# Folding a layer norm into the matrix product behind it: relu output transposed, row statistics added as a product of six rows

## The reference

```python
h = jax.nn.relu(hypergraph_conv(x, adj, W1, b1))   # [512, 512] per graph
h = layer_norm(h, gamma, beta)                     # the inner norm, called Z in the kernel
y = hypergraph_conv(h, adj, W2, b2)                # starts with xw = h @ W2^T, W2^T is [512, 256]
return y + x
```

## Time and profile before

| | us |
|---|---|
| median of 3 runs (range) | 1648.58 (1648.41 to 1649.86) |
| the profiled execution: its own time | 1649.85 |
| the profiled execution: span of the trace | 1648.0 |
| PE busy | 1486.1 (90%) |
| DVE busy | 1146.0 (70%) |
| ACT busy | 908.8 (55%) |
| POOL busy | 284.7 (17%) |
| one turn of the loop | 96.10 |

### The profile page before, as it was taken

How to read it: one execution, slowest core, us unless ns; L and a number is a source line. 1 busy time by engine, 2 the same in 40 slices (tenths; PEclk the granted TensorE clock), 3 DMA queues, 4 the chain that set the end, 5 groups by cost and what they waited for, 6 DMA issues and landing times.

```text
span 1648.0 us, 26778 instructions
## 1 busy us (share of the span) xinstructions
PE 1486.1 (90%) x9850; PEld 1085.8 (66%) x9850; DVE 1146.0 (70%) x2522; ACT 908.8 (55%) x1517; POOL 284.7 (17%) x348
## 2 busy tenths in 40 slices
PE   5688888899899999999999999999999999998986
PEld 4676666667666676766667676666767666676633
DVE  6564766758678686777868677786867778676663
ACT  3424555365565546556554655656465565646564
POOL 3111020202112030210303021030302103120001
PEclk9788999999999999999999999999999999999998
DMA  7010111112120211212021121202112121110021
GB/s 222 1 58 13 52 39 58 39 39 84 58 78 16 74 59 45 76 57 76 15 75 56 45 76 57 76 15 73 58 45 76 57 76 38 45 64 26 1 64 52
DMA packets 58550, 92.17 MB, mean 56 GB/s; under 512 B 4288, under 2 KB 23296, under 8 KB 58496
## 3 DMA queue, kind: packets, MB, share of 16 engines
q1 hardware_dynamic: 58496, 91.44, 17.1%
HBM read 83.04 MB, written 8.39 MB: 55 GB/s over the span
## 4 chain that ended last, share of the span: by engine, by line
PE 55%; issue 20%; DVE 16%; ACT 6%; POOL 2%; DMA 1%; SPq 0%; DVEq 0%; ACTq 0%; POOLq 0%
PE ring_f L1299 33%; PE ring_b L1299 9%; PE ring_b L1569 6%; PE pv_acc L1585 3%; DVE att L1133 3%; DVE bns L928 3%; PE ring_f L1468 2%; POOL rstd L489 2%; DVE rows L1030 2%; ACT hf L568 1%; DVE uz L952 1%; ACT rows L606 1%; DVE m L957 1%; DVE xc_s L952 1%; PE ring_f L1435 1%
## 5 line engine op out<-in xcount | busy, mean ns | idle before, releaser
L1133 DVE TENSOR_TENSOR att<-ring_b,at 128x1024 f32<-128x1024 f32 x256 | 307.2, 1219 | 77.1 <-PE ring_b L1569 69.7
L710 ACT ACTIVATE att<-att 128x1024 f32<-128x1024 f32 x256 | 265.1, 1054 | 136.2 <-DVE att L1133 135.2
L489 POOL TENSOR_TENSOR rstd<-var,mhalf 128x4 f32<-128x4 f32 x80 | 81.3, 1017 | 769.6 <-DVE var L943 769.6
L1299 PE MATMUL ring_f<-w,uz 128*128 128x256 f32 (+1 forms) x896 | 188.9, 333 | 2.3 <-DVE uz L952 1.7
L1299 PE MATMUL ring_f<-m,tr_h 128*128 128x256 f32 x1024 | 190.4, 287 | 0.0
L1299 PEld LDWEIGHTS ring_f<-m,tr_h 128*128 128x128 f32 x1024 | 158.9, 191 | 32.8 <-issue 32.1
L1299 PEld LDWEIGHTS ring_f<-w,uz 128*128 128x128 f32 x896 | 152.0, 192 | 29.8 <-DVE uz L952 12.2
L1585 PE MATMUL pv_acc<-att,xp_n 128*32 128x512 f32 x1024 | 138.5, 617 | 33.9 <-ACT att L710 26.8
L1569 PE MATMUL ring_b<-xc_t,xp_t 32*128 32x512 f32 x1024 | 147.6, 646 | 20.9 <-DVE att L1133 11.7
L1299 PE MATMUL ring_f<-m,inc_n 128*128 128x256 f32 x1024 | 132.2, 288 | 17.8 <-POOL m L493 16.3
L1299 PEld LDWEIGHTS ring_f<-m,inc_n 128*128 128x128 f32 x1024 | 127.0, 195 | 30.6 <-issue 18.7
(11 more groups left out here) (161 smaller groups left out, 2767.8 us busy)
## 6 DMA issues: line engine op xcount, KB each, us to landing
at<-in_adjT SPq DMA_DIRECT2D x32, 1024.0 KB, 5.6
rows<-in_adjT SPq DMA_DIRECT2D x16, 1024.0 KB, 5.5
adj_n<-in_adj SPq DMA_DIRECT2D x16, 1024.0 KB, 5.5
x_in<-in_x SPq DMA_DIRECT2D x16, 512.0 KB, 3.8
out_x<-h SPq DMA_DIRECT2D x16, 512.0 KB, 6.6
wrow<-in_adj SPq DMA_DIRECT2D x16, 256.0 KB, 6.0
att<-in_Wk SPq DMA_DIRECT2D x3, 256.0 KB, 4.2
att<-in_W1T SPq DMA_DIRECT2D x1, 512.0 KB, 9.2
```

The lines of the kernel that those rows point to most:

```text
L489: pool.tensor_tensor(rstd[k][:], var[k][:], mhalf[:], ALU.pow).then_inc(rstd_made[k].sem, 1)
L710: act.activation(v, v, ACT.Tanh).then_inc(tanh_made.sem, 1)
L1133: dve.tensor_tensor(att[:, u % 2, 2 * half:2 * half + 2], ring_b[half][:], at[:, u % NT].unsqueeze(1).broadcast_to([P, 2, N]), ALU.mult).t ...
L1299: ins = pe.matmul(dst, lhsT, rhs, start=(first and n == 0), stop=(last and n == len(pairs) - 1), skip_group_check=True)
```

## The change

The inner norm is no longer applied before the transposes. With r = relu output, mean m and rstd s of a row, z @ W + beta @ W2 = s * (r @ W - m * (gamma @ W2) + (1/s) * (beta @ W2)), where W is W2 with gamma in it. So:

- `f_z` and, for this norm, `offset` are gone; `f_zT` transposes the relu output and waits for `relu_made`.
- A DVE step `f_stat` makes from `sums`, `var` and `rstd` six columns for each node, high and low parts of -m and of 1/s = var*rstd. A PE step `f_stat` transposes them (four transposes of 128x6 into a PSUM bank), ACT `f_stat` copies 6x512 to `stat_t`. In `xw` the product `stat_t` (6 rows) with `rowz` (6 rows: gamma @ W2 and beta @ W2, high and low) takes the place of `sel` with `rowb`, at the head of the last part (k = 3) and not of the first.
- The eviction of xw multiplies by s: ACT and DVE now handle each tile of 128x256 by itself (`scaled`, `scaled_low` with `rstd[Z]` for the factor), as they do for `m` and `m2`.
- The bank table gets an entry v for the new tile (bank 1, between w and n).
- The setup makes `rowz` instead of the first `rowb`, and `set_up_w2` of ACT stands in `f_zT`.
- The lists of all five engines are written anew. In the loop, the units of attention lie one later against the `f` steps; some lists begin a turn at another place.

```diff
-        BANKS = (0, 2, 1, 0, 2, 1, 0, 2, 1, 0, 2, 1, 0, 2, 1, 0, 2, ...)
+        BANKS = (0, 2, 1, 0, 2, 1, 0, 2, 1, 0, 2, 1, 0, 2, 1, 1, 0, 2, ...)
 # ACT
-            def f_z(g, i):
-                if i == 0 and not seen(g, 1):
-                    set_up_w2()
-                normed(g, rows, rows, Z, i, ACT.Identity)
+            def f_stat(g):
+                act.wait_ge(stat_full.sem, stat_full.after(g, 1))
+                if seen(g, 1):
+                    act.wait_ge(xw_full.sem, xw_full.after(g, 2, ago=1))
+                copy(stat_t[0:6], bank_of(ST, 0)[0:6], stat_copied)
-                copy(m1[:, 0, 2 * k:2 * k + 2].rearrange("p t d -> p (t d)"), bank_of(XW, k)[:], xw_hi)
+                scaled(k, bank_of(XW, k), rstd[Z], lambda t: m1[:, 0, t], xw_hi)
 # DVE
+            def f_stat(g):
+                cols = stat[:].rearrange("p t (a k) -> p a t k", a=2)
+                dve.wait_ge(rstd_made[Z].sem, rstd_made[Z].after(g, 1))
+                if seen(g, 1):
+                    dve.wait_ge(stat_full.sem, stat_full.after(g, 1, ago=1))
+                c_stat.begin()
+                dve.tensor_scalar(pair[:, 0], sums[Z][:, :, 0], -0.5, None, ALU.mult)
+                c_stat.link(dve.tensor_tensor(pair[:, 1], var[Z][:], rstd[Z][:], ALU.mult))
+                here(c_stat, g)
+                dve.tensor_copy(cols[:, :, :, 0], pair[:])
+                c_stat.link(dve.tensor_copy(cols[:, :, :, 1], pair[:]))
+                here(c_stat, g)
+                dve.tensor_tensor(cols[:, :, :, 2], pair[:], cols[:, :, :, 0].bitcast(F32), ALU.subtract)\
+                   .then_inc(stat_made.sem, 1)
+                c_stat.end()
-                low(v[:, 1], bank_of(XW, k)[:], v[:, 0], xw_lo)
+                scaled_low(k, bank_of(XW, k), rstd[Z], lambda t: m1[:, 1, t], lambda t: m1[:, 0, t], xw_lo)
 # PE
-                        pe.wait_ge(h_made[Z].sem, h_made[Z].after(g, i + 1))
+                        pe.wait_ge(relu_made.sem, relu_made.after(g, i + 1))
-                    pairs = [(sel[:], rowb[:, 0])] if ks[0] == 0 else []
+                    pairs = [(stat_t[0:6, i * P:(i + 1) * P], rowz[0:6])] if ks[-1] == HT_ - 1 else []
+            def f_stat(g):
+                pe.wait_ge(stat_made.sem, stat_made.after(g, 1))
+                ps = bank(g, ST, 0)
+                for i in range(NT):
+                    ins = pe.transpose(ps[0:6, i * P:(i + 1) * P], stat[:, i].bitcast(F32), ident[:])
+                ins.then_inc(stat_full.sem, 1)
+                    pe.wait_ge(stat_copied.sem, stat_copied.after(g, 1))
 # PE, list of the loop, from the first convolution to the transposes behind y
-                    (2, k_attend, 3), (2, k_scores, 5), (0, f_conv1, 0), (0, f_conv1, 1), (0, f_conv1, 2),
-                    (0, f_conv1, 3), (2, k_attend, 4), (2, k_scores, 6), (2, k_attend, 5), (2, k_scores, 7),
-                    (0, f_zT, 0), (0, f_zT, 1), (1, k_hT), (0, f_zT, 2), (0, f_zT, 3), (0, f_xw, 0), (0, f_xw, 1),
-                    (0, f_xw, 2), (0, f_xw, 3), (2, k_attend, 6), (0, f_m2, 0), (0, f_m2, 1), (2, k_outT, 0),
-                    (2, k_attend, 7), (0, f_y, 0), (2, k_outT, 1), (0, f_y, 1), (1, k_xp, 0), (1, k_xp, 1),
-                    (1, k_xn, 0), (1, k_xc, 0), (0, f_hT, 0), (0, f_hT, 1), (1, k_xc, 1), (1, k_xn, 1), (0, f_sj),
+                    (2, k_attend, 2), (2, k_scores, 4), (0, f_conv1, 0), (0, f_conv1, 1), (0, f_conv1, 2),
+                    (0, f_conv1, 3), (2, k_attend, 3), (2, k_scores, 5), (0, f_zT, 0), (0, f_zT, 1), (0, f_zT, 2),
+                    (2, k_attend, 4), (2, k_scores, 6), (0, f_zT, 3), (0, f_xw, 0), (2, k_attend, 5), (0, f_xw, 1),
+                    (0, f_stat), (2, k_scores, 7), (0, f_xw, 2), (0, f_xw, 3), (2, k_attend, 6), (1, k_hT),
+                    (0, f_m2, 0), (0, f_m2, 1), (2, k_outT, 0), (2, k_attend, 7), (0, f_y, 0), (2, k_outT, 1),
+                    (0, f_y, 1), (1, k_xp, 0), (1, k_xp, 1), (1, k_xc, 0), (1, k_xc, 1), (1, k_xn, 0),
+                    (1, k_xn, 1), (0, f_hT, 0), (0, f_hT, 1), (0, f_sj), (0, f_q, 0), (0, f_q, 1), (2, k_ax, 0, 0),
 # DVE, list of the loop, the same stretch (graph g stands here as 1, because the turn now begins inside it)
+                    (0, bn, 0, 0), (1, f_conv1, 2), (1, bn, 1, 0), (1, f_conv1, 3), (1, bn, 1, 1), (1, bn, 1, 2),
+                    (3, k_unit, 5, 0), (3, k_unit, 5, 1), (1, f_zT, 0), (1, f_zT, 1), (1, bn, 1, 3),
+                    (1, variance, 1), (1, f_zT, 2), (3, k_unit, 6, 0), (3, k_unit, 6, 1), (1, f_zT, 3),
+                    (1, f_stat), (3, k_unit, 7, 0), (3, k_unit, 7, 1), (1, f_xw, 0), (1, f_xw, 1), (1, f_m2, 0),
 # SP, list of the loop
-                    (0, next_x), (2, next_at), (0, next_wrow), (4, store), (2, next_at2), (0, next_adj),
-                    (0, next_adjt),
+                    (0, next_x), (0, next_wrow), (4, store), (2, next_at), (3, next_at2), (0, next_adjt),
+                    (0, next_adj),
```

More of the change, by code:

```diff
@@ L538, in _ @@
+                (-1, k_y, 3),
             )
@@ new lines, in _ @@
+                (0, k_unit, 4, 0), (0, k_unit, 4, 1), (2, bn, 1, 3), (2, variance, 1), (0, k_unit, 5, 0),
+                (0, k_unit, 5, 1), (2, f_zT, 0), (2, f_zT, 1), (0, k_unit, 6, 0), (0, k_unit, 6, 1),
+                (0, k_unit, 7, 0), (0, k_unit, 7, 1), (2, f_stat), (2, f_zT, 2), (2, f_zT, 3), (2, f_xw, 0),
+                (2, f_xw, 1), (0, k_outT, 0), (0, k_outT, 1), (0, bn, 4, 0), (0, bn, 4, 1), (0, bn, 4, 2),
+                (2, f_m2, 0), (2, f_m2, 1), (0, bn, 4, 3), (0, variance, 4), (1, k_hT), (0, offset, 4),
@@ L1642, in turn @@
+                    (2, k_out, 1), (0, f_tt, 0), (0, f_tt, 1), (0, f_tt, 2), (1, k_scores, 0), (0, f_tt, 3),
+                    (0, f_r1), (0, f_r, 0), (1, k_scores, 1), (0, f_r, 1), (1, k_attend, 0), (0, f_x1),
+                    (1, k_scores, 2), (0, f_x2, 0), (0, f_x2, 1),
                 ))
@@ new lines, in _ @@
+                (2, f_xw, 0), (0, k_attend, 7), (2, f_stat), (2, f_xw, 1), (2, f_xw, 2), (2, f_xw, 3),
+                (0, k_outT, 0), (0, k_outT, 1), (2, f_m2, 0), (2, f_m2, 1), (1, k_hT), (2, f_y, 0), (2, f_y, 1),
+                (1, k_xp, 0), (1, k_xp, 1), (1, k_xn, 0), (1, k_xc, 0), (1, k_xn, 1), (1, k_xc, 1), (2, f_hT, 0),
+                (2, f_hT, 1), (2, f_q, 0), (2, f_q, 1), (2, f_sj), (2, f_q, 2), (2, f_q, 3), (0, k_ax, 0, 0),
+                (0, k_ax, 0, 1), (0, k_ax, 1, 0), (0, k_ax, 1, 1), (0, k_out, 0), (0, k_out, 1), (2, f_tt, 0),
@@ new lines, in _ @@
+                (1, k_scores, 5), (3, f_zT, 3), (3, f_xw, 0), (3, f_xw, 1), (1, k_attend, 4), (1, k_scores, 6),
+                (1, k_attend, 5), (3, f_stat), (1, k_scores, 7), (3, f_xw, 2), (3, f_xw, 3), (3, f_m2, 0),
+                (3, f_m2, 1), (3, f_y, 0), (3, f_y, 1), (2, k_hT), (1, k_attend, 6), (1, k_attend, 7),
+                (1, k_outT, 0), (1, k_outT, 1), (2, k_xp, 0), (2, k_xp, 1), (3, f_hT, 0), (3, f_hT, 1),
+                (2, k_xc, 0), (2, k_xc, 1), (3, f_sj), (3, f_q, 0), (3, f_q, 1), (2, k_xn, 0), (3, f_q, 2),
@@ new lines, in _ @@
+                (-1, f_xw, 0), (-1, f_xw, 1), (-1, f_stat), (-3, k_scores, 7), (-1, f_xw, 2), (-1, f_xw, 3),
+                (-3, k_attend, 6), (-2, k_hT), (-1, f_m2, 0), (-1, f_m2, 1), (-3, k_attend, 7), (-3, k_outT, 0),
+                (-3, k_outT, 1), (-1, f_y, 0), (-1, f_y, 1), (-2, k_xp, 0), (-2, k_xp, 1), (-2, k_xn, 0),
+                (-2, k_xc, 0), (-2, k_xc, 1), (-1, f_hT, 0), (-1, f_hT, 1), (-2, k_xn, 1), (-1, f_q, 0),
+                (-1, f_q, 1), (-1, f_sj), (-1, f_q, 2), (-1, f_q, 3), (-3, k_ax, 0, 0), (-3, k_ax, 0, 1),
@@ L1716, in _ @@
+                (-1, k_scores, 5), (-2, k_out, 1), (-1, k_attend, 4), (-1, k_scores, 6), (-1, k_attend, 5),
+                (-1, k_scores, 7), (-1, k_attend, 6), (-1, k_attend, 7), (-1, k_outT, 0), (-1, k_outT, 1),
+                (-1, k_ax, 0, 0), (-1, k_ax, 0, 1), (-1, k_ax, 1, 0), (-1, k_ax, 1, 1), (-1, k_out, 0),
+                (-1, k_out, 1),
             )
```

656 lines of the change are left out of this document (319 added, 337 removed).

## The result

The changed kernel takes 1614.07 us (median, 1613.27 to 1615.91), the kernel before beside it on the same chip 1649.22: a ratio of 0.9786 with a 95% interval of 0.9774 to 0.9798, 35 us or 2.1% less. The forecast was 1626, its range 1606 to 1652. So the direction and the range held, and the gain is 1.55 times the forecast one: 35 us for 22.6.

What follows compares the result with a forecast made beforehand. PE's own work was taken as the bound, 90.84 of a 96.10 us turn. Ten turns at -1.4 (-14), graphs 2, 3, 4 and 15 (-5.6), graph 0 (-2.0) and graph 1 (-1) gave -22.6, so 1626 us, range 1606 to 1652.

Steps and rivals of the forecast that it cites:

- the waits around z: PE's loop waits of 0.71 for the `pv_acc` copy, 1.53 for a tanh and 0.21 for z; -2.45 us a turn.
- `xp_t`: PE's wait for `xp_t` in the loop, claimed to go because xc follows `xp 1`; -0.78 us a turn.
- The waits that the prediction adds up to 4.98: PE's loop waits: three around z, one for `xp_t`, two at transposes behind y, one for ax's low part; 4.98 us.
- The wait at the statistics step: PE waiting for `stat_made` at the new transposes, between 0 and 0.8 us a turn; 0.4 taken.
- The walk: Convolution to `f_stat` in the new order: PE 11.4 us, DVE 11.5, so they arrive together.
- Rival (b): DVE takes PE's place before `f_stat`; 2 us late means a wait of 2.4 a turn and 1659 us; chance 0.16.
- The wait at `sj`: PE waiting at `f_sj`, which now follows the last `hT` with nothing between; 0.9 us a turn.
- The transposes: Four new PE transposes of the statistics columns, overlapping; 0.5 us a graph, bounds 0.43 and 0.88.
- Rival (d): The new transposes do not overlap, 0.27 each, 1.1 us instead of 0.5; 1636 us; chance 0.04.
- The product of six rows: Four six-row products in xw replace four bias products; no gain or loss, bounds four times 0.1 us either way.
- The loop together: Sum of the terms for one loop turn, -1.4 us; ten turns -14, a turn of 94.7 us.
- The first graphs: Start to third `k_out`, -7.2 us: 2.0 saved in graph 0, 1 in graph 1, 1.4 each in graphs 2 to 4.

Runs made afterwards that it cites:

- e1: The changed kernel's computation with the order of the kernel before on every engine; 1700.87 us against 1650.56 for the kernel before, ratio 1.0300.
- e2: The computation of the kernel before in the changed kernel's order, its output not the reference's; 1702.83 us, 1.0322 of the kernel before.
- e5: The changed kernel with one batch-statistics instruction more on VectorE, result unread, just ahead of the statistics step; 1625.55 us, 0.9850 of the kernel before.
- e6: The changed kernel with three batch-statistics instructions more on VectorE (1.9 us) just ahead of the statistics step; 1639.48 us, 0.9945 of the kernel before.
- e3: The changed kernel with the statistics product over 128 rows in place of 6, the added rows zero; 1597.66 us, 0.9678 of the kernel before.
- e10: The changed kernel with the statistics product over 32 rows in place of 6, the added rows zero; 1613.78 us, 0.9786 of the kernel before.
- e4: The changed kernel with one xc product moved behind the hT transposes and the xn transposes forward, also in graphs 1, 2, 4, 15; 1611.46 us, 0.9764 of before.
- e11: The changed kernel with the statistics product over 128 rows and, in the loop alone, one xc product moved behind the hT transposes; 1594.32 us, 0.9662 of before.

## Why the prediction was right, and where it was short

**What falls away in the loop: right in size, half right in cause.** -2.45 for the waits around z and -0.78 for `xp_t` were both measured as gone. The text gave ScalarE's 2.93 us on z and VectorE's full list as the reason for the first. e1 shows that the waits of 0.71 and 1.53 stay when the 2.93 are gone: they were the order's. The fold was needed so that the order without them would not wait 3.91 for the norm (e2). The 0.78 went with the order in e2 too. (The waits that the prediction adds up to 4.98 make 4.96.)

**The wait at the statistics step: 0.4 forecast, none measured.** The walk gave PE 11.4 us and VectorE 11.5 from the last convolution; they took 11.64 and 11.17. VectorE is 0.47 ahead. That the forecast wait is missing hangs on so little: with one instruction of 0.6 to 0.7 us more on VectorE (e5) the turn already grows by 0.2. Rival (b) was the right thing to fear: with 1.9 us more on VectorE the turn grows by 1.35 and 25 us of the 35 are lost (e6).

**The wait at `sj`: 0.9 forecast, 1.07 measured**, and with it a cost that no term had: the clock dips, 1.54 us in four of ten turns.

**The transposes: 0.5 forecast, 0.52 measured.** Rival (d), 0.27 each, is out. Their records last 0.27 and overlap, as those of z did. By the Trainium skill's 275 ns for one (TensorE: Matmul & The Clock Gate, Part 4: PE-mode transpose) an estimate for four would be 1.1; the measurement decides.

**The product of six rows: nothing forecast, with bounds of 0.4 either way; 1.13 us a turn measured** (94.48 to 93.35 in e3), 16 us in all. This is the term that was mis-sized, and its bound failed. The argument was that the scores with 32 rows have no shorter records than others. But they come in eights, and a change is paid once at the ends of a group, where no record shows it. Here lone products of six rows stood between products of 128, six changes more a turn.

**The loop together.** Forecast -1.4 a turn, measured -1.6 without the dips and -1.0 with them. Forecast turn 94.7 with 91.3 us of PE, measured 94.48 with 91.67. With the terms as measured (-3.23, +1.07, +0.52, +1.14) the sum would be only -0.5; the other 1.1 us came in beside them. 0.3 is in waits under 0.1. The rest is PE's busy time: the new computation in the old order (e1) raises it by 1.7 a turn, 90.84 to 92.53, and the new order takes 0.86 of that off again. The likely reason, argued and not tested, is that each wait costs more than its idle time: the product behind it has its whole record of 0.28 to itself, where the next start would come after 0.12. With four waits less than e1, at 0.16 each, that is 0.64, and one change of rows less (`rowz` behind the scores) is 0.19. The same reckoning makes e1 2.2 us busier than before (0.52, seven changes, an eighth lying in its wait of 0.77, and two waits more), where it is 1.7, so the split of this 0.86 stays open. That the loop came out near the forecast although one term was 1.1 too low is in this part luck.

**The first graphs: -7.2 forecast, -24.2 measured.** This is why the gain is larger than forecast. Windows of before and of the changed kernel up to the first `k_out`:

```profile
0.00:276.83 276.83, 214.50 (x1296) 171.14 (x1296) 171.29 (x435) 122.45 (x212) 48.39 (x61) 0.90 0.18 57
```

```profile
0.00:259.79 259.79, 206.35 (x1309) 164.70 (x1309) 170.00 (x447) 115.94 (x206) 50.23 (x61) 0.95 0.19 62
```

Of the 17.0 us, 8.9 are idle time of PE (62.3 to 53.4) and 8.1 are busy time, with 13 instructions more, at a clock of 0.95 for 0.90. The forecast has 4.4 up to there (2 for graph 0, 1 for graph 1, 1.4 for graph 2). The step that failed is to have counted there a few waits alone, at full clock: the idle time fell by twice that, and the clock gave as much again. By the starts of like products the changed kernel is 2.8 us ahead at graph 0's product with `inc_t` behind m2 (forecast 2), 10.4 at graph 1's, and 17.0 at the first `k_out`. The forecast named the clock of these graphs as a risk of loss only. How much clock a wait costs there is not settled: e5 loses 7.0 us with new waits of 0.75, 0.29 and 0.36 at the stat transposes of graphs 0 to 2, and e10 loses 1.9 with none of them. Six other kernels that keep all the work and have this order in the first graphs, up to the move in e4, put the first `k_out` at 257.4 to 261.7, so the gain itself stands. The two stretches behind it, to the third `k_out`, gave another 7.2 (100.74 to 96.43 and 97.76 to 94.89), where before waited 2.81 and 0.82 for tanh in the first and 1.72 in the second. Which of the many moved steps saves how much in these five graphs was not separated: e2 has the first `k_out` at 269.54 with the order alone, e1 at 281.89 with the computation alone, and together it is 259.79; so up to there the order alone does gain, 7.3 of the 17.0, with an output that is not the reference's.

## What to carry to other kernels

Where an edit shortens a dependency chain, the gain may only be there for the order that the shorter chain allows, so cost the two together, and test each alone before naming a cause. Keep the number of rows of neighbouring products equal, by zero rows or by putting the odd ones in a row; the record of a group doesn't tell what a lone one costs. Where PE is near its bound, look also at runs of transposes and waits of a few us: here the clock fell behind them in some turns and not in others, and one product between ended it (none in 20 turns). Because the fall comes and goes, read its cause from several traces and not from one. Before work is moved into a gap, look at who must free its bank.

## What the runs showed that was not expected

- A change between products of 6 or 32 rows and products of 128 costs 0.19 us in the stream, either way. Six and 32 rows cost the same (1614.07 and 1613.78); 128 rows, or the six-row products in a row, give 1597.66 and 1595.82.
- The granted clock fell behind 3.86 us of transposes and waits in 4 of 10 turns of the same code (20 of 70 over seven kernels with this order) and in none of 20 once a product of 1.03 us stood between; the low stretch costs 1.54 us each time.
- In graph 1 the clock fell behind the stat transposes in four of ten kernels (the changed one and e3 to e11), in two of them with the waits of the changed kernel (1.6 us lost) and in two with a longer wait there (2.9 and 3.0 us).
